# Graph attention and a routed feed-forward on one core: degrees by way of DRAM, and two pairs of heads at once in the graph layers

## The chip, the core and the metric

The kernel runs on one core of a Trainium2 chip. The metric is the time of one execution on the device in microseconds (us), as a median of several. Engines are named as the profile names them: PE (TensorE, its weight loads PEld), DVE (VectorE), ACT (ScalarE), POOL (GpSimd) and SP (SyncE, which here only issues DMAs). Each engine runs its own list of instructions strictly in order and waits on semaphores for the others.

## What is computed

Sixteen batches of 256 tokens of width 128 go through an attention block with a graph network in it, and then through a mixture of eight experts of which each token takes two. All is float32.

```python
xn = layer_norm(layernorm(x), gamma_in)
q, k, v = (xn @ Wq) * scale, xn @ Wk, xn @ Wv        # 16 heads of 64
attn = softmax(causal(q @ k.T))
out  = attn @ v
adj  = clip(attn + eye, 0, 1)
deg  = adj.sum(-1)
feats = v
for l in range(2):
    h = adj @ (feats @ gnn_w[l] + gnn_b[l]) / deg
    feats = gelu(h + feats)
out = out + feats @ lin_w + lin_b
x = x + layer_norm(out @ Wo, gamma_out)
# then: x + alpha * (top-2 of 8 experts: silu(gate) * up, down) of rmsnorm(layernorm(x))
```

The graph matrix that the kernel uses is adj / deg. Since only the diagonal of adj differs from attn, the attention output is recovered from the mixed values: attn @ v = deg * ((adj / deg) @ v) - (something on the diagonal), which the kernel arranges as (mixed values minus v) times the degree.

## The kernel before

**Stages.** A prologue loads the weights and splits them into high and low parts. Then one batch after another goes through `batch(b, before, routed, after)`: b is the batch in hand, `before` the batch whose attention output is being finished and normalised (b-1), `routed` the one whose tokens are sent to the experts' slots in DRAM (b-2), `after` the next, whose input is normalised. Batches 0, 1 and 15 are written out, 2 to 14 are a loop on every engine (`Fori`). Last, `sorted_stage` runs the experts over 71 tiles of sorted tokens, and the results are fetched and added.

**A batch.** Its 16 heads are 8 pairs n; a pair's two heads lie on the two halves of the partitions. Per pair: PE projects queries and keys (`queries_keys`), then `scores` (two banks of a rotation of three: `scores(n)` waits for `exps(n-1, 0)`); DVE takes the row maxima (`maxima`); ACT takes exponentials with their sums (`exps`); DVE puts in the diagonal and sums the degree parts (`adjacency`, then the reciprocal in `weights`); POOL scales the rows (`graph`, lines 497 and 499); PE transposes the result (`transposes`), ACT copies it to SBUF (`graph` on ACT, gt0 and gt1).

**Mixed values and degrees.** `differences` on PE multiplies the graph matrix with the values into the left half of bank 5. For the degree POOL multiplies den and rs, each value spread over 64 columns (`degrees`, line 508: 128x256 outputs a pair, tile deg), and PE transposes that with two 128x128 transposes (`degrees`, line 774) into the right half of bank 5. DVE then makes dT = bank - vT (`difference`, L1435) and aT = bank * dT (`attended`, L1440), and ACT copies the mixed values (`mixed_values`, gvT). Each of these has 256 columns.

**The two graph layers.** Again pair by pair with 256 columns in a bank: `layer1` (PE), `layer1_out` (DVE, adds vT, L1455), `gelu1` (ACT), `layer2_in` (PE, four instructions of 128 columns), its copy (ACT, g1), `layer2` (PE), `layer2_out` (DVE, adds f1T, L1461), `gelu2` (ACT), `output_graph` (PE). The first tiled step of the output, `output_start`, and `output_attended` go into bank 7 with `output_graph`; `output_bias` and `output_kept` (DVE) take it out, with `output_natural` (PE) between.

**The order** is written out by hand in one `batch` function for each engine. Nothing plans it at run time: a call that isn't ready holds all that is behind it on its engine. The page's line 635 is the helper that issues every product; groups are told apart by their tiles.

**DVE's small steps** are spread between: `norm_step` 0 to 5 (next batch's input), `norm_tokens` 0 to 11 (batch before), `choose`, `place_tokens` (routing), and in the last batch `table_first` and `gate_up_high` (the experts' weights, whose low parts are POOL's `gate_up_low`).

**SP** issues the loads, then 33 DMAs that fill the slots in DRAM with zeros (line 364), then the experts' weights, and nothing between there and the last batch's loads.

Of the kernel before, what the change touches and what calls it, by code (L numbers as in the profile page):

```python
# [19 lines left out]
P = 128  # L20
BATCHES, TOKENS, DIM = 16, 256, 128
HEADS, DHEAD = 16, 64
PAIRS = HEADS // 2
TILES = TOKENS // P
# [48 lines left out]
def build_program(nc, x, wq, wk, wv, wvT, gnn_w, gnn_b, lin_wT, lin_b, wo, gamma_in, gamma_out,  # L73
                  norm_w, routerT, guT, downT, alpha, slots, pairs, out):
# [9 lines left out]
    with ctx:  # L84
# [26 lines left out]
        sq4 = sb("sq4", [P, TILES, DIM])  # L111
# [12 lines left out]
        zero = sb("zero", [P, CLEAR * ROW])  # L124
# [35 lines left out]
        gu_lo = sb("gu_lo", [P, EXPERTS, 2 * HID], f32r)  # L160

# [18 lines left out]
        deg = at("deg", [P, 3, 4, DHEAD])  # L180
# [4 lines left out]
        gvT = at("gvT", [P, PAIRS, TOKENS])  # L185
        vT = at("vT", [P, PAIRS, TOKENS])
        aT = at("aT", [P, PAIRS, TOKENS])
        f1T = at("f1T", [P, 4, TOKENS])
        g1 = at("g1", [P, 2, TILES, P])
        dT = at("dT", [P, TOKENS])  # L190
        z1 = at("z1", [P, 2, TOKENS])
        z2 = at("z2", [P, 2, TOKENS])
        f2T = at("f2T", [P, 4, TOKENS])
# [14 lines left out]
        xn = at("xn", [P, TILES, DIM])  # L208
# [48 lines left out]
        p_deg = Signal(sem("p_deg"), PAIRS)  # L257
# [3 lines left out]
        a_d = Signal(sem("a_d"), PAIRS)  # L261
        d_d = Signal(sem("d_d"), PAIRS)
        s_deg = Signal(sem("s_deg"), PAIRS)
        d_a = Signal(sem("d_a"), PAIRS)

        s_f1, d_z1 = Signal(sem("s_f1"), PAIRS), Signal(sem("d_z1"), PAIRS)
        a_f1 = Signal(sem("a_f1"), PAIRS)
        s_g1, a_g1 = Signal(sem("s_g1"), PAIRS), Signal(sem("a_g1"), PAIRS)
        s_h2, d_z2 = Signal(sem("s_h2"), PAIRS), Signal(sem("d_z2"), PAIRS)
        a_f2, s_og = Signal(sem("a_f2"), PAIRS), Signal(sem("s_og"), PAIRS)  # L270
# [46 lines left out]
        L1_BANK, L2_IN_BANK, L2_BANK = 0, 2, 1  # L317
        MIX, DEG = slice(0, TOKENS), slice(TOKENS, 2 * TOKENS)
# [17 lines left out]
        def _(sp):  # L336
# [24 lines left out]

            sp.wait_ge(k_consts, 1)
            for r in range(0, SLOT_ROWS, CLEAR * P):
                sp.dma_start(slots[r:r + CLEAR * P, :].rearrange("(p r) d -> p (r d)", p=P),
                             zero[:, :]).then_inc(w_clear, 16)

# [7 lines left out]
            for e in range(EXPERTS):  # L374
                if e >= 2:
                    sp.wait_ge(k_gu_lo, e - 1)
                sp.dma_start(raw_gu[:, e % 2, :], guT[e]).then_inc(w_gu[e % 2], 16)
# [54 lines left out]
        def _(pool):  # L432
# [70 lines left out]
            def degrees(b, n):  # L503

                s = n % 3
                if n >= 3:
                    s_deg.wait(pool, b, n - 2)
# [1550 lines left out]
```

## Time and profile before

| | us |
|---|---|
| median of 3 runs | 1147.88 |
| lowest, highest | 1142.15, 1152.14 |
| the profiled execution | 1155.31 |
| its span, first to last instruction | 1153.4 |
| PE busy | 1071.1 (93%) |
| DVE busy | 884.1 (77%) |
| ACT busy | 803.4 (70%) |
| POOL busy | 500.3 (43%) |

The profiled execution is 0.65% above the median, and its span is 1.9 us less than its time. "Busy" is time covered by at least one instruction; matmuls overlap in the pipeline, so the mean duration of one is longer than the distance from one start to the next, and it is the distance between starts that tells what a step costs PE.

### The profile page before, as it was taken

The numbers are of one execution on the slowest core, as the hardware profiler recorded it, in microseconds if no ns is written. First come the engines' busy times: TensorE is split into PE (matmuls) and PEld (weight loads), VectorE is DVE, ScalarE is ACT, GpSimd is POOL, SyncE is SP. The second block draws the span as 40 slices with busy tenths as digits, with TensorE's granted clock in tenths as the row PEclk, the third lists the DMA queues.
The fourth block names the chain that finished last, engine by engine and source line by source line (L and its number), as shares of the span: only waits on it lengthen the run. The fifth ranks groups of instructions, "written<-read, shape, count | busy, mean of one in ns | idle before, by whom it ended". The sixth has DMA issues, their size and how long they took to land.

```text
span 1153.4 us, 28732 instructions
## 1 busy us (share of the span) xinstructions
PE 1071.1 (93%) x8576; PEld 854.7 (74%) x8576; DVE 884.1 (77%) x3760; ACT 803.4 (70%) x2351; POOL 500.3 (43%) x649
## 2 busy tenths in 40 slices
PE   4899999999999999999999999999999968898993
PEld 3777777777777777777777777777777747898993
DVE  3667797979797979797979797979797984565556
ACT  3668686868686868686868686868787735464551
POOL 3334244434343535353534353535353552544444
PEclk9899999999999999999999999999999988998997
DMA  6970000000000000000000000000000021222227
GB/s 192 405 260 2 1 2 11 1 10 1 10 1 11 1 10 0 10 0 10 0 10 0 10 0 10 0 10 0 10 0 10 2 78 44 56 57 61 59 61 226
DMA packets 37312, 47.43 MB, mean 41 GB/s; under 512 B 6009, under 2 KB 28539, under 8 KB 37200
## 3 DMA queue, kind: packets, MB, share of 16 engines
q1 hardware_dynamic: 32880, 37.81, 10.3%
q0 software_dynamic: 4320, 8.47, 2.2%
q14 instruction: 84, 0.69, 0.2%
q8 instruction: 28, 0.46, 0.2%
HBM read 18.14 MB, written 28.58 MB: 41 GB/s over the span
## 4 chain that ended last, share of the span: by engine, by line
PE 83%; DVE 6%; issue 3%; ACT 2%; SPq 2%; DMA 1%; another core or an unknown queue 1%; POOL 0%; DVEq 0%; POOLq 0%; ACTq 0%
PE bank L635 68%; PE bank L735 3%; PE bank L748 3%; PE bank L774 2%; PE bank L751 2%; PE bank L749 2%; PE bank L1006 2%; DMA x_all<-in_x 1%; PE bank L988 1%; DVE eb L1421 1%; DVE x_all L1995 1%; DVE got L1993 1%; DVE nmax L1406 0%; PE bank L783 0%
## 5 line engine op out<-in xcount | busy, mean ns | idle before, releaser
L497 POOL TENSOR_TENSOR ea<-ea,wgt 128x256 f32<-128x256 f32 x128 | 80.0, 625 | 429.6 <-DVE wgt L1430 396.1
L1406 DVE TENSOR_REDUCE nmax<-bank 128x1 f32<-128x128 f32 (+1 forms) x512 | 152.2, 347 | 66.0 <-PE bank L635 57.1
L499 POOL TENSOR_TENSOR eb<-eb,wgt 128x512 f32<-128x512 f32 x128 | 133.6, 1044 | 0.0
L635 PE MATMUL bank<-gt,g 128*64 128x256 f32 (+1 forms) x1024 | 112.0, 339 | 19.5 <-DVE z L1461 12.0
L1421 DVE SCALAR_TENSOR_TENSOR eb<-idw,ssum,eb 128x256 f32<-128x256 f32 x256 | 129.8, 544 | 0.0
L1124 ACT ACTIVATE ea<-bank,nmax 128x128 f32<-128x128 f32 x256 | 95.8, 374 | 47.9 <-DVE nmax L1406 45.9
L1124 ACT ACTIVATE eb<-bank,nmax 128x256 f32<-128x256 f32 x256 | 123.4, 482 | 0.0
L1092 ACT ACTIVATE gt<-bank 128x512 f32<-128x512 f32 (+1 forms) x256 | 111.7, 493 | 13.3 <-PE bank L751 11.8
L635 PE MATMUL bank<-gt,vnat 128*64 128x256 f32 (+1 forms) x1024 | 110.0, 335 | 3.0 <-issue 0.8
L635 PE MATMUL bank<-qk 64*128 64x128 f32 (+1 forms) x1024 | 112.7, 339 | 0.0
L525 POOL DMA_INDIRECT pairs<-zout,zin x71 | 69.7, 981 | 99.0 <-DVE zout L1954 89.3
L635 PEld LDWEIGHTS bank<-gt,g 128*64 128x64 f32 x1024 | 66.5, 137 | 61.4 <-issue 35.4
L1092 ACT ACTIVATE g<-bank 128x256 f32<-128x256 f32 x128 | 48.8, 381 | 84.8 <-PE bank L635 84.8
L635 PEld LDWEIGHTS bank<-gt,vnat 128*64 128x64 f32 x1024 | 65.1, 136 | 50.2 <-issue 17.0
L1461 DVE TENSOR_TENSOR z<-bank,f1T 128x256 f32<-128x256 f32 x128 | 53.6, 419 | 48.5 <-PE bank L635 48.5
L635 PE MATMUL bank<-xt_lo,w_hi 128*128 128x256 f32 x256 | 87.0, 340 | 1.9 <-DVE xt_lo L1399 1.9
L635 PE MATMUL bank<-gw,f1T 128*128 128x128 f32 x512 | 88.1, 295 | 0.3 <-ACT f1T L1148 0.3
L1947 DVE TENSOR_TENSOR shid<-bank,ssg 128x352 f32<-128x352 f32 x71 | 37.3, 525 | 63.5 <-ACT ssg L1272 40.6
L1092 ACT ACTIVATE qk<-bank 128x512 f32<-128x512 f32 x128 | 78.1, 610 | 11.2 <-PE bank L635 8.9
L635 PEld LDWEIGHTS bank<-gw,f1T 128*128 128x128 f32 x512 | 70.3, 192 | 19.3 <-issue 11.0
L1418 DVE SCALAR_TENSOR_TENSOR ea<-ident,ssum,ea 128x128 f32<-128x128 f32 x256 | 83.2, 362 | 0.0
L1092 ACT ACTIVATE gvT<-bank 128x256 f32<-128x256 f32 x128 | 49.1, 383 | 44.2 <-DVE aT L1440 40.6
(234 smaller groups left out, 3153.0 us busy)
## 6 DMA issues: line engine op xcount, KB each, us to landing
slots<-zero SPq DMA_DIRECT2D x33, 520.0 KB, 15.0
zin<-slots SPq DMA_DIRECT2D x71, 65.0 KB
got<-pairs SPq DMA_DIRECT2D x8, 512.0 KB, 5.5
raw_gu<-in_guT SPq DMA_DIRECT2D x8, 352.0 KB, 3.0
out<-x_all SPq DMA_DIRECT2D x8, 256.0 KB, 2.7
pairs<-zout,zin POOLq DMA_INDIRECT x71
dn<-in_downT SPq DMA_DIRECT2D x2, 512.0 KB, 16.0
slots<-z,row_now POOLq DMA_INDIRECT x64
```

The source lines that it names most:

```text
L497: nc.gpsimd.tensor_tensor(ea[:, s], ea[:, s], wgt[:, s, 0:2].unsqueeze(2).to_broadcast([P, 2, P]), ALU.mult)
L499: nc.gpsimd.tensor_tensor(eb[:, s], eb[:, s], wgt[:, s, 2:4].unsqueeze(2).to_broadcast([P, 2, 2 * P]), ALU.mult).then_inc(p_g.sem, 1)
L525: nc.gpsimd.indirect_dma_start(pairs, bass.IndirectOffsetOnAxis(ap=zin[:, j % RING, ID:ID + 1].bitcast(u32), axis=0), zout[:, j % RING, :] ...
L635: return nc_mm(o, st, mo, start=first, stop=last, **more)
L735: mm = nc.tensor.transpose(o[:, m * TOKENS + t * P:m * TOKENS + (t + 1) * P], vnat[:, t, n * P:(n + 1) * P], ident[:, :])
L1092: return nc.scalar.activation(o, i, ACT.Copy, **more)
L1124: done = nc.scalar.activation(e[:, s, a, :], score_bank(n, a)[:, TILE_SCORES[t]], ACT.Exp, bias=nmax[:, s, i:i + 1], accum_out=ssum[:, s, ...
L1406: done = V.tensor_reduce(nmax[:, n % 3, i:i + 1], score_bank(n, a)[:, TILE_SCORES[t]], X, ALU.max, negate=True)
L1418: V.scalar_tensor_tensor(ea[:, s, a, :], ident[:, :], ssum[:, s, a:a + 1], ea[:, s, a, :], ALU.mult, ALU.max, accum_out=den[:, s, a:a + 1])
L1421: done = V.scalar_tensor_tensor(eb[:, s, a, :], idw[:, :], ssum[:, s, 2 + a:3 + a], eb[:, s, a, :], ALU.mult, ALU.max, accum_out=den[:, s, ...
L1461: V.tensor_tensor(z2[:, n % 2, :], bank[L2_BANK][:, 0:TOKENS], f1T[:, n % 4, :], ALU.add).then_inc(d_z2.sem, 1)
L1947: V.tensor_tensor(shid[:, j % 2, 0:HID], bank[2 + j % 2][:, 0:HID], ssg[:, j % 2, :], ALU.mult).then_inc(d_hid.sem, 1)
```

## The change

1. **Degrees.** POOL multiplies four values a partition for a pair (tile dg) and no longer 256. SP writes them, two pairs (one "double") at a time, to a DRAM tensor `degs` as rows of 512 tokens, and reads each row back onto 64 partitions at once (tile dgb, four buffers). PE's transposes of deg and deg itself are gone. The product with the degree, `attended`, now has both its inputs in SBUF (aT and dgb), and runs in place.
2. **Doubles.** `differences`, `difference`, `attended`, `mixed_values`, `layer1`, `layer1_out`, `gelu1`, `layer2_in`, `layer2`, `layer2_out` and `gelu2` each take two pairs, in a whole bank of 512 columns. The last double uses banks 4 and 3 in layer 2. As before, `layer2(d)` waits for `layer2_out(d-1)` whichever bank it writes.
3. **Order anew** on PE, ACT, DVE and POOL. DVE's `attended(0)` comes in the second half of the batch, `attended(1)` and `attended(2)` after the last `layer2_out`, and `attended(3)` in the next batch behind its first maxima; so `output_attended` 0 to 7 all go to the next batch. POOL's `deviation` and `degrees` come earlier or later, and its `token_power(before, 0)` after graph(7) and degrees(7).
4. **SP** issues 9 of the 33 zero fills at once and three more behind each of the first eight doubles; the degree DMAs of batches 2 to 15 follow the loads of the experts' weights 0 and 1, and those of weights 2 to 7 come after them.
5. Tiles: `zero` lies in gu_lo, xh is normalised in place (xn is gone), sq4 is gone, gvT has 4 pairs for 8.

```diff
-        deg = at("deg", [P, 3, 4, DHEAD])
+        dg = at("dg", [P, DOUBLES, 2, 2, TILES])
+        dgb = at("dgb", [P, DGB, 2 * TOKENS])
...
+            def degrees_out(k):
+                p_dg.wait(sp, k // DOUBLES, 2 * (k % DOUBLES) + 2)
+                sp.dma_start(degs[2 * k:2 * k + 2, :].rearrange("a (j p) -> p (a j)", p=P),
+                             dg[:, k % DOUBLES].rearrange("p a m t -> p (a m t)"),
+                             allow_slow_non_contiguous=True).then_inc(w_dg[k % 2], 16)
+            def degrees_in(k):
+                sp.wait_ge(w_dg[k % 2], 16 * (k // 2 + 1))
+                if k >= DGB:
+                    sp.wait_ge(d_a.sem, k - DGB + 1)
+                for a in range(2):
+                    sp.dma_start(dgb[a * DHEAD:(a + 1) * DHEAD, k % DGB, :],
+                                 degs[2 * k + a:2 * k + a + 1, :].to_broadcast([DHEAD, 2 * TOKENS])).then_inc(w_dgb[k % DGB].sem, 16)
+            def degrees(first, last):
+                for k in range(first, last):
+                    degrees_out(k)
+                    if k % DOUBLES:
+                        degrees_in(k - 1)
+                    if k % DOUBLES == DOUBLES - 1:
+                        degrees_in(k)
...
             def degrees(b, n):                                     # POOL
-                nc.gpsimd.tensor_tensor(deg[:, s], den[:, s, :].unsqueeze(2).to_broadcast([P, 4, DHEAD]),
-                                        rs[:, s, :].unsqueeze(2).to_broadcast([P, 4, DHEAD]),
-                                        ALU.mult).then_inc(p_deg.sem, 1)
+                nc.gpsimd.tensor_tensor(dg[:, n // 2, :, n % 2, :].rearrange("p a t -> p t a"),
+                                        den[:, s, :].rearrange("p (t a) -> p t a", t=TILES),
+                                        rs[:, s, :].rearrange("p (t a) -> p t a", t=TILES),
+                                        ALU.mult).then_inc(p_dg.sem, 1)
...
-            def differences(b, n):                                 # PE
+            def differences(b, d):
+                a_gt.wait(pe, b, 2 * d + 2)
+                if d >= 1:
+                    a_d.wait(pe, b, d)
+                for m in range(2):
+                    n = 2 * d + m
+                    mm = mixed(bank[5][:, m * TOKENS:(m + 1) * TOKENS],
+                               lambda t, a: vnat[:, t, n * P + a * DHEAD:n * P + (a + 1) * DHEAD], n)
+                mm.then_inc(s_mix.sem, 1)
-            def degrees(b, n):
-                p_deg.wait(pe, b, n + 1)
-                for t in range(TILES):
-                    mm = nc.tensor.transpose(
...
+            def layer2(b, d):
+                a_g1.wait(pe, b, d + 1)
+                if L2_BANKS[d] in (3, 4):
+                    a_gt.wait(pe, b, PAIRS)
+                if d >= 1:
+                    d_z2.wait(pe, b, d)
...
+            def attended(b, d):                                    # DVE
+                d_d.wait(dve, b, d + 1)
+                w_dgb[d].wait(dve, b, 32)
+                V.tensor_tensor(aT[:, 2 * d:2 * d + 2, :], aT[:, 2 * d:2 * d + 2, :],
+                                dgb[:, d % DGB, :].rearrange("p (n i) -> p n i", n=2), ALU.mult).then_inc(d_a.sem, 1)
```

PE's second part of the batch, as it now stands:

```diff
+                scores(b, 7)
+                places(routed, bank[7][:, PLACES], before)
+                differences(b, 1)
+                layer1(b, 0)
+                transposes(b, 5)
+                layer1(b, 1)
+                x_transposed(after, b)
+                output_start(b, before, routed)
+                layer2_in(b, 0)
+                differences(b, 2)
+                layer2(b, 0)
+                transposes(b, 6)
+                layer2_in(b, 1)
+                transposes(b, 7)
+                layer1(b, 2)
+                differences(b, 3)
+                layer2(b, 1)
+                output_graph(b, 0)
+                layer1(b, 3)
+                output_graph(b, 1)
+                layer2_in(b, 2)
+                queries_keys(after, 0, b)
+                output_graph(b, 2)
+                layer2_in(b, 3)
+                layer2(b, 2)
+                layer2(b, 3)
+                tokens_transposed(before, bank[6], after)
+                queries_keys(after, 1)
+                output_graph(b, 3)
+                values(after, 0, b)
```

DVE, from the seventh pair's maxima on:

```diff
+                weights(b, 5)
+                maxima(b, 7, 0)
+                take_places(routed, bank[7][:, PLACES])
+                maxima(b, 7, 1)
+                place_tokens(routed, 0)
+                place_tokens(routed, 1)
+                difference(b, 1)
+                norm_tokens(before, 0)
+                layer1_out(b, 0)
+                norm_step(after, 5)
+                adjacency(b, 6)
+                adjacency(b, 7)
+                weights(b, 6)
+                norm_tokens(before, 1)
+                layer1_out(b, 1)
+                difference(b, 2)
+                weights(b, 7)
+                layer2_out(b, 0)
...
+                layer2_out(b, 3)
+                attended(b, 1)
+                attended(b, 2)
```

## Rows read from the trace of the kernel before

**Rows 1.** Busy time by stretch: length, then PE, PEld, DVE, ACT, POOL, PEclk, DMA, GB/s
```profile
195.94:252.90 56.96, 56.10 (x464) 43.17 (x464) 47.63 (x217) 43.71 (x134) 24.95 (x33) 1.00 0.02 5
...
824.40:881.40 57.00, 56.13 (x465) 43.19 (x464) 47.63 (x217) 43.75 (x134) 24.96 (x33) 1.00 0.02 5
...
541.96:570.96 29.00, 28.89 (x259) 22.46 (x258) 25.51 (x123) 25.12 (x85) 10.49 (x15) 1.00 0.00 1
570.96:599.00 28.04, 27.28 (x209) 20.78 (x209) 22.10 (x95) 18.66 (x49) 14.48 (x19) 1.00 0.03 10
```

**Rows 2.** PE in order of time, one batch of the loop: start, duration, instruction
```profile
562.57 0.88 PE L635 MATMUL bank<-qk 64*128 64x128 f32 x8
563.38 0.39 PE L635 MATMUL bank<-xt_lo,w_hi 128*128 128x256 f32 x1
...
564.28 0.87 PE L635 MATMUL bank<-gt,vnat 128*64 128x256 f32 x8
...
573.25 0.33 PE L748 MATMUL bank<-ident,ea 128*128 128x128 f32 x1
...
573.96 0.60 PE L635 MATMUL bank<-gvT,gw 128*128 128x256 f32 x2
574.40 0.38 PE L774 MATMUL bank<-ident,deg 128*128 128x128 f32 x2
574.62 1.03 PE L635 MATMUL bank<-aT,wo_sb 128*128 128x256 f32 x4
575.48 0.68 PE L635 MATMUL bank<-gw,f1T 128*128 128x128 f32 x4
576.04 0.70 PE L635 MATMUL bank<-aT,wo_sb 128*128 128x256 f32 x2
...
577.10 0.87 PE L635 MATMUL bank<-gt,vnat 128*64 128x256 f32 x8
577.80 0.82 PE L635 MATMUL bank<-gt,g 128*64 128x256 f32 x8
578.55 0.71 PE L635 MATMUL bank<-gw,f1T 128*128 128x128 f32 x4
```

**Rows 3.** DVE in order of time, same batch, and past the loop's end
```profile
540.75 0.43 DVE L1461 TENSOR_TENSOR z<-bank,f1T 128x256 f32<-128x256 f32 x1 [1.94 <-PE bank L635]
543.73 1.15 DVE L1406 TENSOR_REDUCE nmax<-bank 128x1 f32<-128x128 f32 x4 [2.55 <-PE bank L635]
...
572.54 0.41 DVE L1455 TENSOR_TENSOR z<-bank,vT 128x256 f32<-128x256 f32 x1
...
885.21 1.15 DVE L1406 TENSOR_REDUCE nmax<-bank 128x1 f32<-128x128 f32 x4 [1.83 <-PE bank L635]
```

**Rows 4.** Instructions on tile x_all: min/median/max ns, first and last start
```profile
L1995 DVE TENSOR_TENSOR x_all<-x_all,got x6: 691/692/2062, 1137.8 to 1148.9; 128x512 f32<-128x512 f32 x6
```

**Rows 5.** DVE and POOL in order of time: one held instruction and its neighbour
```profile
578.10 1.25 DVE L1421 SCALAR_TENSOR_TENSOR eb<-idw,ssum,eb 128x256 f32<-128x256 f32 x1
...
579.28 0.48 DVE L1421 SCALAR_TENSOR_TENSOR eb<-idw,ssum,eb 128x256 f32<-128x256 f32 x1
...
579.69 0.41 DVE L1455 TENSOR_TENSOR z<-bank,vT 128x256 f32<-128x256 f32 x1
580.02 0.41 DVE L1461 TENSOR_TENSOR z<-bank,f1T 128x256 f32<-128x256 f32 x1
...
577.99 1.08 POOL L499 TENSOR_TENSOR eb<-eb,wgt 128x512 f32<-128x512 f32 x1
```

**Rows 6.** DMA issues by line: KB each, median us to landing
```profile
slots<-zero SPq DMA_DIRECT2D x33, 520.0 KB, 15.0
...
gb<-in_gnn_b SPq DMA_DIRECT2D x4, 0.2 KB, 2.3
```

**Rows 7.** The last batch's longest wait on PE, and ACT's table load
```profile
931.39 1.55 PE L635 MATMUL bank<-gt,g 128*64 128x256 f32 x8 [5.10 <-DVE z L1461]
...
573.59 1.28 ACT L1148 ACT_TABLE_LOAD   x1
```

More of the change, by code:

```diff
@@ L565, in batch @@
                         scatter(routed, c)
+                graph(b, 6)
+                graph(b, 7)
                 degrees(b, 6)
-                graph(b, 7)
                 degrees(b, 7)
-                if after is not None:
-                    deviation(after, 1, 7)
+                if before is not None:
+                    token_power(before, 0)
                 if after is None:
-                    for e in range(0, 3):
+                    for e in range(0, 2):
                         gate_up_low(e)
@@ L796, in layer2_in @@
-            def layer2_in(b, n):
-                a_f1.wait(pe, b, n + 1)
-                if n >= 1:
-                    a_g1.wait(pe, b, n)
-                for t in range(TILES):
-                    mm = product(bank[L2_IN_BANK][:, xt(t)], f1T[:, n % 4, xt(t)], gw[:, 1, :], True, True)
-                mm.then_inc(s_g1.sem, 1)
-            def layer2(b, n):
-                a_g1.wait(pe, b, n + 1)
-                if n >= 1:
-                    d_z2.wait(pe, b, n)
-                mixed(bank[L2_BANK][:, 0:TOKENS],
-                      lambda t, a: g1[:, n % 2, t, a * DHEAD:(a + 1) * DHEAD], n).then_inc(s_h2.sem, 1)
+                    d_z1.wait(pe, b, d)
@@ new lines, in layer1, with layer2_in @@
+                for m in range(2):
+                    mm = product(bank[L1_BANK][:, m * TOKENS:(m + 1) * TOKENS], gw[:, 0, :], gvT[:, 2 * (d % 2) + m, :],
+                                 True, True)
+                mm.then_inc(s_f1.sem, 1)
+            def layer2_in(b, d):
+                a_f1.wait(pe, b, d + 1)
+                if L2_IN_BANKS[d] in (3, 4):
+                    a_gt.wait(pe, b, PAIRS)
+                if d >= 1:
+                    a_g1.wait(pe, b, d)
+                for i in range(2 * TILES):
+                    mm = product(bank[L2_IN_BANKS[d]][:, xt(i)], f1T[:, d % 2, xt(i)], gw[:, 1, :], True, True)
+                mm.then_inc(s_g1.sem, 1)
@@ L870, in batch @@
                     folded_lin(1)
+                if before is not None:
+                    output_graph(before, 6)
+                    output_attended(before, 3)
                 scores(b, 4)
-                differences(b, 1)
+                transposes(b, 1)
                 if before is not None:
-                    output_natural(before)
-                degrees(b, 1)
+                    output_graph(before, 7)
+                    output_attended(before, 4)
                 queries_keys(b, 6)
@@ L880, in batch @@
                 scores(b, 5)
+                differences(b, 0)
+                transposes(b, 3)
+                if before is not None:
+                    output_attended(before, 5)
+                scores(b, 6)
+                if before is not None:
+                    output_attended(before, 6)
+                    output_attended(before, 7)
                 queries_keys(b, 7)
-                differences(b, 2)
+                transposes(b, 4)
+                if before is not None:
+                    output_natural(before)
@@ L1252, in tokens_transposed @@
+                if after is not None:
+                    values(after, 0)
             def tokens_transposed(p, o):
```

569 lines of the change are left out of this document (238 added, 331 removed).

## The prediction

> **What bounds the kernel now.** I read the stretches by batch first. Batches of the loop are alike: from 195.94 to 881.40 us there are 12, 57.12 us each, and in each PE is busy for 56.1, DVE 47.6, ACT 43.8, POOL 25 [rows 1]. The clock is granted in full (1.00, 2.4 GHz) throughout, so it is no lever. PE is the bound, by its own work and not by a chain; sixteen batches make some 920 of the 1153 us, and the change touches nothing else but the start and the passage to the experts. Then the two parts of a batch: from `scores(0)` to the end of `scores(7)` (541.96 to 570.96, 29.0 us) DVE is busy for 25.5; in the rest (28.0 us) for 22.1 [rows 1]. So DVE is close behind PE in the first part: `layer1_out(1)` starts at 572.54, 1.6 us after `scores(7)` ended [rows 3]. A change that makes PE's batch shorter runs into DVE soon. That decides this case.
>
> **What PE saves.** Degree transposes: two of them move the next start by 0.22 us (574.40 to 574.62) [rows 2]; their mean of 0.28 each is overlap and not what they cost. Eight pairs: 8 x 0.22 = 1.8 us a batch. Doubles: a mixed group of eight costs 0.70 where another follows (577.10 to 577.80) and 0.75 where another kind does; after queries and keys the distance from the last start is longer still [rows 2]. The new order has 12 such runs of narrow groups where the old has 16. At 0.05 to 0.3 a run I take 0.2, 0.8 us in all. `layer2_in` doesn't gain: four instructions cost 0.56 (575.48 to 576.04) [rows 2] and eight will cost 1.1; nor does `layer1`, 0.44 each. PE's own need is 56.1 - 1.8 - 0.8 = 53.5 us.
>
> **What the others save.** One 512-column instruction for two of 256. On DVE two steps follow at 0.33 (579.69 to 580.02) [rows 5], a mean of 0.42; one of 512 columns takes 0.69 [rows 4], 0.61 from start to start. So 32 of 0.34 become 16 of 0.61: 10.9 to 9.8 us, 1.1 a batch. ACT saves some 3 us and POOL, whose degree product shrinks from 256 outputs to 4, some 3 more (bounds 0 and 5); neither is the bound at 44 and 25 of 57 [rows 1], so I count nothing for them.
>
> **DVE's walk through the new order** (0 is the start of `scores(0)`). Before, from the first maximum to `layer1_out(1)` passed 572.54 - 543.73 = 28.8 us [rows 3], of which DVE idled 29.0 - 25.5 - 1.77 (its late start) = 1.7 [rows 1, 3]: 27.1 of work. The new order takes out of this stretch nine 256-column steps (3.1) and a norm step (0.4), and puts in `difference(0)`, `attended(3)` of the batch before (1.2) and three norm steps (1.3): 26.1. With small waits of 0.4, 26.5.
>
> When does it start? Before, the last step of a batch ended at 541.18 and the first maximum began at 543.73, 2.55 us later, though its scores ended at 542.96; past the loop's end the same wait was 1.83 [rows 3]. I read the 2.55 as the price of DVE's own turn of the loop. It was hidden, for DVE's last step ended before `scores(0)` began. Now `attended(1)` and `attended(2)` stand between the last `layer2_out` and the turn, 1.2 us more. PE does 2.2 us (tokens, queries and keys, graph output, values) between the end of `layer2(3)` and `scores(0)`; `layer2_out(3)` takes 0.6 to 0.7 of these; so DVE begins at -1.5 + 1.2 + 2.55 = 2.2 us, where it was 1.77. Then maxima(7) end at 2.2 + 26.5 = 28.7; behind them come `place_tokens` (0.9), `difference(1)` (0.6), `norm_tokens(0)` (0.4) and `layer1_out(0)` (0.6): 31.2. With `output_kept`, for which `places` waits, and the held small steps, 31.7.
>
> PE's work up to `layer1(1)`, which waits for that: eight scores at 0.93 (the 0.81 of 562.57 to 563.38 and the masks' 0.12) 7.4, six projections at 0.85 5.1 (563.38 to 564.28 is 0.90), values 2.4, value transposes 1.8, six `transposes` at 0.71 (573.25 to 573.96) 4.2, twelve output products at 0.43 (574.62 to 575.48 are two) 5.2, two double differences 3.0, `layer1(0)` 0.9, small ones 0.7: 30.7 [rows 2]. So PE waits there about 1.0 us.
>
> **After `layer1(1)`** PE has: six double mixed groups (`differences` 2 and 3, `layer2` 0 to 3) at 1.5 each (0.70 + 0.80) 9.0; `transposes` 6 and 7 1.4; three `layer1` 2.6; four `layer2_in` 4.4; output graph 1.7; projections and values of the next batch 2.3; start of output and two transposed pairs 1.1 [rows 2]: 22.5. New stalls: `layer2(3)` stands right behind `layer2(2)` but waits for `layer2_out(2)`, drain, 0.69 [rows 4] and hand-over, 0.85 us; `layer2_in(0)` waits for a table load of 1.28 [rows 7] and gelu, over which PE has 1.8 of work, 0.3; `differences(3)` waits for POOL's graph(7), transposes and ACT's copy, 0.1 or 0.2. Together 23.9. POOL's `token_power(before, 0)` now stands behind graph(7): DVE's `norm_tokens(2)` waits for it some 1.3 us, covered since `layer1_out(2)` can't start before `layer1(2)`. `transposes(6)`, for which POOL must first be through with its four scatters, has 0.4 to 1 us of room.
>
> **Sum.** 31.7 + 23.9 = 55.6, say 55.7 us a batch against 57.12: 1.4 less. Thirteen turns of the loop: 18. Batches 0 and 1 have no turn and less DVE work, 1.8 each (the transposes): 3.6. Start: DVE waits for x either way, one adjacency fewer stands before the second pair's maxima: 1. The last batch: before, PE lost 5.10 us in one wait for `layer2_out` [rows 7]. Now `attended` 1 to 3, `table_first(4)` behind `gate_up_high(7)` and SP's loads behind the last degrees come late; between a gain of 5 and a loss of 10 I take a loss of 3. Total -20 us (18 + 4 + 1 - 3). The profiled execution's 1155 would become 1135; from the median of 1147.9 I forecast 1128 us, own range 1116 to 1142.
>
> **DMAs.** A double's degrees leave as 512 elements of 4 bytes. No row shows that many; bounds are 2.3 us (64 elements) and 15.0 (520 KB behind others) [rows 6]. I take 3 to 4 for the write and 3 for the read, 7 with issue. SP is idle in between, and issues 12 a batch at some 0.5. `attended(3)` has the least room: degrees(7) are there some 7.5 us after `layer1(1)` starts, it is wanted at 3 to 4 of the next batch, 19 us later. The others have as much or more. The 24 zero fills spread over batches 0 and 1 delay only reads with that room. Nothing counted.
>
> **A rule of the skill that speaks against the change.** A DVE step that began at 578.10 beside POOL's 577.99 product took 1.25 us where the next of its kind, at 579.28, took 0.48: it was held [rows 5]. The Trainium skill, "SBUF — State Buffer", on which engine shares which port, says that a DVE instruction with two SBUF inputs and a GpSimd instruction that reads SBUF exclude each other for the whole of one of them. The trace agrees, with 0.77 us lost. Before, `attended` read a bank; now both its inputs are in SBUF. From the row alone: one of the four, `attended(0)`, stands beside a product of POOL, +0.8 us where DVE isn't last; the other three are beside an idle POOL. I count nothing, and the held steps go into a rival.
>
> **Rivals.**
> 1. *PE stays the bound.* If the 2.55 us are a wait for something else, or DVE catches up, the batch comes to 53.5 plus 0.85 and little else, 54.3: 2.8 x 13 = 36, + 5 - 3: 1110; without any stall 1100. For it: 1.7 us of idle DVE in the first part, and ACT's and POOL's relief. Against: 26.5 us of DVE work in a PE stretch of 27 to 28. I give 1104. Chance 0.18.
> 2. *DVE gives it all back.* Held steps (the 0.77), a turn of 2.85, exps late behind the table load: 1.2 to 1.4 us more per batch on the path to `layer1_out(0)`. Then 57 us a batch, and 1147. Chance 0.20.
> 3. *The degrees come late* (the slower side). Place: `attended(3)`, at the head of DVE's batch, with maxima and everything behind it. It decides from a round trip of 19 us on; each microsecond over is one per batch. Two landings near 10 us, with issue 21 to 22, give 2.5 x 15 = 37 on top of 1128: 1165. Elements of 4 bytes speak for it, an otherwise empty queue (DMA share 0.02 [rows 1]) against. With longer DVE chains of the same effect, chance 0.13.
>
> **Numbers.** Forecast 0.49. About 1% (11 us) is what a measurement here tells from no change, so faster means below 1136. Of the forecast 0.42 lies there, of rival 1 all, nothing of the others: 0.60. Same: 0.07 + 0.19 = 0.26. Slower: 0.14. The range 1098 to 1152 leaves out rival 3 and the edges.
>
> **What will show it.** In the profile after: a loop batch of 55 to 56.5 us, PE busy 53 to 54; L774 gone; DVE's 512-column steps at 0.69; a PE wait for z of L1455's successor (`layer1_out(0)`) near 1 us and one for `layer2_out(2)` near 0.85 in each batch; the first maxima 2 us or more after `scores(0)` began. Wrong if `attended` waits for DMA, if DVE idles over 2 us in the first part, or if the batch is under 54.5 or over 57.

## The result, and the profile after

The changed kernel takes 1211.24 us (median of 4 runs, 1205.77 to 1215.33) against 1147.78 (4 runs): the ratio is 1.0549, 95% interval [1.05, 1.0598]. The forecast was 1128 us, with a range of 1098 to 1152; the kernel became slower and not faster, and its time lies outside the range. The profiled execution has a span of 1207.3 us against 1153.4. The kernel before was measured anew beside each group of runs below (medians of 1145.99 to 1154.04 us), and each ratio is against that; medians of different groups can differ by some 0.5% for that reason alone.

First the page of the changed kernel: the busy row, then the DMA rows (packets, MB, share of the 16 engines over the span).

```profile
PE 1030.5 (85%) x8320; PEld 833.0 (69%) x8320; DVE 859.0 (71%) x3504; ACT 767.4 (64%) x2095; POOL 444.9 (37%) x649
DMA packets 114053, 63.99 MB, mean 53 GB/s; under 512 B 74617, under 2 KB 97147, under 8 KB 114000
q1 hardware_dynamic: 109680, 54.87, 34.9%
q0 software_dynamic: 4320, 8.47, 6.3%
q14 instruction: 26, 0.21, 0.1%
```

The same DMA rows of the kernel before:

```profile
DMA packets 37312, 47.43 MB, mean 41 GB/s; under 512 B 6009, under 2 KB 28539, under 8 KB 37200
q1 hardware_dynamic: 32880, 37.81, 10.3%
q0 software_dynamic: 4320, 8.47, 2.2%
q14 instruction: 84, 0.69, 0.2%
```

No engine does more work than before. What grew is the number of packets: 64 doubles of 1024 pieces of 4 bytes are 65,536, nearly all of the 68,600 more below 512 B. And the scatters' queue (q0), with the same 4320 packets, is three times as busy.

Where the 53.9 us went, by the starts of `scores(0)` (the first `mask,pick` row of a batch on TensorE): up to batch 3 217.4 us against 198.7 (+18.7); the 12 batches from there 58.62 each against 57.12 (+18.0); from batch 15 to the end 286.6 against 269.2 (+17.4). A third in each.

The loop first. Two of its batches in their two parts, up to `scores(7)` and from there, as in [rows 1] (columns: stretch, length, then PE, PEld, DVE, ACT and POOL busy, clock, DMA share, GB/s):

```profile
507.69:535.73 28.04, 26.71 (x223) 20.78 (x223) 23.50 (x119) 23.09 (x78) 9.77 (x15) 1.00 0.02 0
535.73:566.26 30.53, 26.36 (x225) 20.72 (x226) 23.17 (x83) 18.43 (x41) 11.77 (x18) 1.00 0.71 36
566.26:596.06 29.80, 26.72 (x223) 20.78 (x223) 23.50 (x119) 23.10 (x78) 9.76 (x15) 1.00 0.04 9
596.06:629.47 33.41, 27.68 (x226) 21.50 (x227) 22.08 (x83) 18.30 (x41) 11.74 (x18) 0.95 0.59 40
```

PE is busy for 53.1 us of the first batch (53.5 were forecast), DVE for 46.7. The batches are no longer alike: 58.6 and 63.2 us here, 55.6 to 63.2 over the loop. DMA engines that had a share of 0.02 over a batch [rows 1] have 0.6 to 0.7 in the second part. TensorE's clock plays a small part: it is granted in full (2.4 GHz) in the whole loop before, and in the changed kernel but for three stretches of 3.4 us at half (1.2 GHz), which is why the last row has 0.95. They lie in the three longest batches (61.8, 63.2 and 62.7 us), and the one in the rows, from 597.3 to 600.7, follows a wait of TensorE of 2.9 us. By an estimate from these figures they cost 1.7 us each at most, 5 of the 36 us that the loop takes more than in the run without the DMAs below.

Now TensorE's waits for VectorE in the first of these batches, and the first maximum of the next:

```profile
541.15 1.10 PE L664 MATMUL bank<-gvT,gw 128*128 128x256 f32 x4 [0.73 <-DVE z L1471]
562.61 1.52 PE L664 MATMUL bank<-gt,g 128*64 128x256 f32 x16 [0.88 <-DVE z L1479]
567.31 0.62 DVE L1417 TENSOR_REDUCE nmax<-bank 128x1 f32<-128x128 f32 x2 [1.25 <-PE bank L664]
```

`layer1(1)` waits 0.73 us for `layer1_out(0)` (forecast 1.0) and `layer2(3)` 0.88 for `layer2_out(2)` (forecast 0.85). VectorE's first maximum comes 1.05 us after `scores(0)` began and not at 2.2, with 1.25 of idle time in place of the 2.55 of [rows 3]. So the two foreseen waits of TensorE are there in about their size. The lost time is elsewhere, in the list of waits (us in total, times, longest):

```profile
DVE aT L1455 <- DMA dgb<-degs: 21.8, 6, 10.6
POOL ea L525 <- DMA slots<-gu_lo: 18.1, 1, 18.1
DVE gu_hi L1486 <- DMA raw_gu<-in_guT: 17.6, 4, 15.7
DVE z L1479 <- remote: 16.1, 9, 3.3
DVE nmax L1417 <- remote: 14.6, 8, 3.4
ACT gt L1115 <- remote: 12.9, 7, 3.1
```

and in SyncE's own:

```profile
SPq L367 <- POOL dg L535: 501.7, 32, 21.4
SPq L376 <- DMA degs<-dg: 192.5, 33, 11.7
```

A write of degrees (L367) lands up to 11.7 us after SyncE begins to wait for it; 3 to 4 us were forecast. The first three waits of the engines belong to the start and the end: `attended` of the first batches for late degrees, the first scatter (for which GpSimd holds `ea`) for zero fills (their source tile is now `gu_lo`) that SyncE issued between degrees, and the last batch for gate and up weights that stand behind the last degrees in SyncE's queue. Those with the releaser "remote" are the loop's for the most part: the profile writes this where a signal came but no instruction that gives it had ended in the 1.5 us before. Here is the largest, in order of time:

```profile
589.12 0.28 PE L664 MATMUL bank<-mask,pick 64*128 64x128 bf16 x4
589.24 0.87 PE L664 MATMUL bank<-qk 64*128 64x128 f32 x8
589.83 0.69 DVE L1447 TENSOR_TENSOR aT<-bank,vT 128x512 f32<-128x512 f32 x1
593.87 1.15 DVE L1417 TENSOR_REDUCE nmax<-bank 128x1 f32<-128x128 f32 x4 [3.35 <-remote]
594.53 0.37 ACT L1147 ACTIVATE ea<-bank,nmax 128x128 f32<-128x128 f32 x1 [4.06 <-DVE nmax L1417]
595.47 0.44 PE L811 MATMUL bank<-ident,yT 128*128 128x128 f32 x2 [2.93 <-DVE yT L1460]
```

`scores(6)` is through at 590.1, and VectorE, free from 590.5, takes the maxima at 593.9. A second place, 17 us on:

```profile
606.33 1.47 PE L664 MATMUL bank<-gt,g 128*64 128x256 f32 x16
608.22 0.38 PE L784 MATMUL bank<-ident,eb 128*128 128x128 f32 x2
610.96 0.69 DVE L1479 TENSOR_TENSOR z<-bank,f1T 128x512 f32<-128x512 f32 x1 [3.19 <-remote]
611.03 0.87 ACT L1115 ACTIVATE gt<-bank 128x512 f32<-128x512 f32 x2 [2.71 <-remote]
```

`layer2(0)` ended at 607.8 and `transposes(6)` at 608.6; VectorE and ScalarE, which wait for them, both start at 611.0. All lines of this kind in the loop are waits for a group of TensorE. The kernel before has none in its loop.

The trace also has the time of each semaphore signal, and it tells on which side the delay is. For the first place: four groups of TensorE ended at 590.1, 591.2, 591.9 and 592.5, and their signals are recorded at 593.85, 593.91, 593.98 and 594.06, all within 0.21 us and in the order of the groups. From 200 to 880 us, 50 of TensorE's 702 recorded signals come more than 1 us after the end of their group, the worst 3.7 us; of the 1773 signals of VectorE, ScalarE and GpSimd none comes later than 0.02 us. So VectorE starts at once when its signal comes, and TensorE's signals come late (or its matmuls end late: the ends in the profile are modelled).

### The profile page after: what moved, and what is told of

Same layout as the page of the kernel before. It is cut to its first block, busy times and chain, and to the rows that moved or that the text cites. A ratio compares the mean times of both kernels' runs of the same rounds, so it can differ in the third digit from the quotient of the medians.

```text
span 1207.3 us, 27665 instructions
## 1 busy us (share of the span) xinstructions
PE 1030.5 (85%) x8320; PEld 833.0 (69%) x8320; DVE 859.0 (71%) x3504; ACT 767.4 (64%) x2095; POOL 444.9 (37%) x649
## 3 DMA queue, kind: packets, MB, share of 16 engines
q0 software_dynamic: 4320, 8.47, 6.3%
## 4 chain that ended last, share of the span: by engine, by line
issue 41%; POOL 18%; PE 17%; DMA 15%; DVE 3%; SPq 3%; ACT 1%; POOLq 0%; another core or an unknown queue 0%; DVEq 0%; ACTq 0%
PE bank L664 13%; DMA slots<-z,row_now 7%; POOL eb L527 7%; POOL slots L547 4%; POOL ea L525 3%; DMA degs<-dg 3%; PE bank L1024 2%; POOL rstd L519 1%; POOL dg L535 1%; SPq L376 1%; DMA dgb<-degs 1%; DMA pairs<-zout,zin 1%; DMA x_all<-in_x 1%; DMA zin<-slots 1%; DMA raw_gu<-in_guT 1%
## 5 line engine op out<-in xcount | busy, mean ns | idle before, releaser
L664 PE MATMUL bank<-gt,g 128*64 128x256 f32 (+1 forms) x1024 | 98.4, 335 | 19.5 <-DVE z L1479 16.8
L1433 DVE SCALAR_TENSOR_TENSOR eb<-idw,ssum,eb 128x256 f32<-128x256 f32 x256 | 113.5, 480 | 0.0
L664 PE MATMUL bank<-gt,vnat 128*64 128x256 f32 (+1 forms) x1024 | 100.8, 341 | 6.2 <-ACT gt L1115 3.6
L664 PE MATMUL bank<-gw,f1T 128*128 128x128 f32 x512 | 71.1, 282 | 26.2 <-ACT g L1115 21.6
L1479 DVE TENSOR_TENSOR z<-bank,f1T 128x512 f32<-128x512 f32 x64 | 43.9, 686 | 64.9 <-PE bank L664 48.8
L664 PEld LDWEIGHTS bank<-gw,f1T 128*128 128x128 f32 x512 | 65.2, 193 | 32.5 <-ACT f1T L1174 25.1
L664 PE MATMUL bank<-aT,wo_sb 128*128 128x256 f32 x256 | 80.5, 410 | 7.3 <-DVE aT L1455 7.3
L781 PE MATMUL bank<-ident,ea 128*128 128x128 f32 x256 | 66.2, 286 | 18.0 <-ACT gt L1115 12.9
L1174 ACT ACTIVATE f1T<-z,gb 128x512 f32<-128x512 f32 x64 | 46.1, 721 | 55.6 <-DVE z L1471 47.2
L664 PE MATMUL bank<-gvT,gw 128*128 128x256 f32 x256 | 69.4, 394 | 13.5 <-DVE z L1471 9.4
```

Source lines behind the costliest of these rows:

```text
L664: return nc_mm(o, st, mo, start=first, stop=last, **more)
L781: nc.tensor.transpose(bank[3][:, a * TOKENS:a * TOKENS + P], ea[:, s, a, :], ident[:, :])
L1174: nc.scalar.activation(f1T[:, d % 2, :], z1[:, d % 2, :], ACT.Gelu, bias=gb[:, 0:1]).then_inc(a_f1.sem, 1)
L1433: done = V.scalar_tensor_tensor(eb[:, s, a, :], idw[:, :], ssum[:, s, 2 + a:3 + a], eb[:, s, a, :], ALU.mult, ALU.max, accum_out=den[:, s, ...
L1479: V.tensor_tensor(z2[:, d % 2, :], bank[L2_BANKS[d]][:, :], f1T[:, d % 2, :], ALU.add).then_inc(d_z2.sem, 1)
```

## The experiments

In each diff "-" is the changed kernel's line, unless said otherwise.

**Without the DMAs.** Does the new order hold what it promised?

```
-                    degrees_out(k)
-                    if k % DOUBLES:
-                        degrees_in(k - 1)
...
-                w_dgb[d].wait(dve, b, 32)
```

> The changed kernel without any of its 192 degree DMAs: attended multiplies by a tile of ones that is set once, and waits for no DMA (the output lacks the degrees). Theory A (the degree DMAs do the harm: their many 4-byte pieces hold up whatever else goes through the same DMA engines, and with it DVE and ACT, whose idle stretches of 1.2 to 3.4 us have no engine as releaser): a loop batch falls from 58.6 to 55.5 to 56.5 us, the stretches before maxima(6) and layer2_out(0) go, and with the start and the last batch mended the time is near 1125. Theory B (the new order and the doubles are slow by themselves, the stretches belong to the loop's own code): the loop batch stays at 58 or above and only start and end are mended, some 1180.

Measured: 1131.96 us (2 runs), ratio 0.9822 [0.9744, 0.99]. The twelve batches from batch 3 on are alike to 0.03 us; one of them:

```profile
468.26:523.83 55.57, 52.81 (x448) 41.50 (x448) 46.38 (x201) 41.48 (x118) 21.53 (x33) 1.00 0.01 5
```

55.57 us where 55.7 were forecast. The 79 us between the changed kernel and this run are due to the DMAs of the degrees.

**The same DMAs in the kernel before** (of a spare tile, for batches 2 to 14; its degree transposes stay):

```
+            for k in range(8, 60):
+                degrees_out(k)
+                if k % 4:
...
+                    degrees_in(k - 1)
```

> The kernel before with the same DMAs beside it in batches 2 to 14: for each double one write of 1024 pieces of 4 bytes and two reads of 128 KB onto 64 partitions, of a spare tile, for which no engine waits but SP. Theory A: the loop batch of the old order grows from 57.1 by 1.5 to 3 us, time 1165 to 1185. Theory B: it stays within 0.3 us of 57.1, time within 1% of before.

Measured: 1236.37 us, ratio 1.0728 [1.062, 1.0836]: more than expected. Its loop batches take 63.2 us in place of 57.1, and its waits say "remote" as well (35.8 us at `nmax`, 24.2 at `z`). The old order suffers more, 6.1 us a batch against 3.0; why isn't shown. The harm needs no degree that comes late, for nothing reads them here.

**128 pieces of 32 bytes.**

```
-                sp.dma_start(degs[2 * k:2 * k + 2, :].rearrange("a (j p) -> p (a j)", p=P),
+                sp.dma_start(degs[2 * k:2 * k + 2, :].rearrange("a (q f) -> (a q) f", f=8),
```

> The changed kernel, whose writes of degrees go out as 128 runs of 32 bytes and not as 1024 of 4 bytes (the reads are the same in size and number, the values land in another order, so the output is another). Theory A in its narrow form (it is the number of tiny pieces): loop batch near 56, time 1140 to 1160, since the round trip is short in the first batches and the last too. If the reads (256 KB a double) or the round trip itself do it, the loop batch stays over 58.

Measured: 1138.61 us, ratio 0.988 [0.979, 0.9969]; loop batches 55.85. The 128 reads of 128 KB are still there: they are not the cause.

**Writes only.**

```
-                        degrees_in(k - 1)
+                        sp.wait_ge(w_dg[(k - 1) % 2], 16 * ((k - 1) // 2 + 1))
...
-                w_dgb[d].wait(dve, b, 32)
+                Signal(w_dg[d % 2], 32).wait(dve, b, 16 * (d // 2 + 1))
```

> The changed kernel with the writes of 4-byte pieces left as they are and the broadcast reads left out; attended waits for the landing of its write and multiplies by ones, so the output lacks the degrees. Theory A1 (the 1024 small pieces of a write do the harm alone): 1180 to 1215 us, with the same idle stretches of VectorE at the maxima of pair 6. Theory A2 (they do it only where they meet the reads and scatters): 1132 to 1160 us.

Measured: 1206.3 us, ratio 1.0495 [1.0436, 1.0554]: theory A1. The writes do it, without the reads. The queues of this run from 524 to 566 us:

```profile
q0 software_dynamic: 128, 0.27, 20.1%
q1 hardware_dynamic: 4160, 0.02, 4.5%
```

and of the run without degree DMAs from 540 to 600:

```profile
q0 software_dynamic: 128, 0.27, 1.3%
```

The 128 packets of four scatters keep the engines busy for 0.201 x 42 = 8.4 us of their time in place of 0.013 x 60 = 0.8. The 4096 pieces themselves take only 1.9: it is others that they make slow.

**Other sizes.** 256 pieces of 16 bytes, with the broadcast row read at a stride by `attended`; 512 of 8 bytes likewise:

```
+                sp.dma_start(degs[2 * k:2 * k + 2, :].rearrange("a (p f) -> p a f", p=P),
+                             dg[:, k % DOUBLES].rearrange("p a m t -> p a (m t)")).then_inc(w_dg[k % 2], 16)
...
+                now = aT[:, 2 * d:2 * d + 2, :].rearrange("p n (t i) -> p n t i", t=TILES)
+                V.tensor_tensor(now, now, dgb[:, d % DGB, :].rearrange("p (i n t) -> p n t i", n=2, t=TILES),
```

> The changed kernel with each double's degrees written as 256 pieces of 16 bytes instead of 1024 of 4 bytes; DRAM then holds them token by token, the broadcast reads are as before, and attended takes the degrees at a stride of 4 elements. It computes all that the reference does. Theory A (what costs is the number of small pieces): near the run with 128 pieces of 32 bytes, 1135 to 1150 us. Theory B (what costs is that pieces below some size, here under 32 bytes, are slow each): half or more of the loss stays, over 1165 us. The strided operand of attended could cost up to 0.7 us a double if it halves VectorE's rate, which would show as a mean of 1.3 us in place of 0.68.

> The changed kernel with each double's degrees written as 512 pieces of 8 bytes, the point between 1024 pieces (1211 us) and 256 pieces (1133 us). If the harm grows with the number of pieces in proportion beyond those of 16 bytes: (512 - 256) / (1024 - 256) of the 78 us, 1159 us. If there is a limit above which the transfers no longer hide: below 1140 or above 1180 us.

Measured: 16 bytes 1132.8 us, ratio 0.9878 [0.9844, 0.9912]; 8 bytes 1138.13 us, 0.9872 [0.9845, 0.9898]. Not in proportion: 512 pieces of 8 bytes and 256 of 16 cost little, 1024 of 4 bytes cost 79 us. With 16 bytes `attended` reads the degrees at a stride of four elements, with 8 bytes at a stride of two. Their rows:

```profile
L1455 DVE TENSOR_TENSOR aT<-aT,dgb 128x512 f32<-128x512 f32 x64 | 69.0, 1100 | 0.0
L1455 DVE TENSOR_TENSOR aT<-aT,dgb 128x512 f32<-128x512 f32 x64 | 42.7, 690 | 0.0
```

The stride of four made it slower, 1100 ns in place of 684, and the batch is 55.84 us in place of 55.57; the stride of two cost `attended` nothing (690).

**Turned on TensorE first**, so that a double leaves as 8 rows of 512 bytes:

```
+                nc.tensor.transpose(bank[4][0:8 * (last - first), 2 * P:3 * P],
+                                    dg[:, first:last].rearrange("p d a m t -> p (d a m t)"),
```

> The changed kernel with the degrees turned on TensorE first (3 transposes of 128 columns a batch, into the free part of bank 4, copied by ScalarE into a tile of 16 partitions), so that a double's degrees leave as 8 rows of 512 bytes. It computes all that the reference does. Theory A (pieces): no waits for DMA in the loop, batches of 55.8 plus up to 0.9 us (3 transposes of 0.3 on TensorE), in all 1132 to 1150 us. If instead the transfers harm by being there at all, whatever their pieces: over 1165 us.

Measured: 1146.07 us, ratio 0.999 [0.9973, 1.0006]. The pieces are gone and so is the gain: batches are 56.3 us (0.7 more than without DMAs, which three transposes may explain), and `attended` waits 17.3 us in all for degrees that take one more stage.

**Number, size or place?**

```
(512 of 4 bytes)    degs[2 * k:2 * k + 1, :] ... dg[:, k % DOUBLES, 0]
(8 bytes, twice)    the write of 8 bytes, and once more to rows 2 * (k + BATCHES * DOUBLES)
(64 bytes apart)    degs[k % 2:k % 2 + 1, :].rearrange("o (j p s) -> p (o j) s", p=P, s=16)[:, :, 0]
(8 bytes apart)     the same with s=2
```

> As the run with writes only (no reads, attended multiplies by ones, so the output lacks the degrees), with only one head's half of each double's degrees written: 512 pieces of 4 bytes in place of 1024 (1206 us). If their number in a write has a limit between 512 and 1024: 1128 to 1145 us. If it is the size of 4 bytes, each piece with its own cost: half the harm, near 1169 us.

> The kernel with 512 pieces of 8 bytes, with each double's degrees written twice, to two places of DRAM: 1024 pieces in two writes. If the number of pieces is what harms: as with 1024 of 4 bytes, over 1180 us. If the size of 4 bytes does: within 10 us of 1138.

> As the run with writes only, the 1024 pieces of 4 bytes lying 64 bytes apart in DRAM in place of side by side (attended multiplies by ones, so the output lacks the degrees). If neighbours that fall into the same few bytes of DRAM hold each other up: under 1160 us. If each piece of 4 bytes costs by itself wherever it lies: 1195 to 1215 us.

> As the run with writes only and pieces 64 bytes apart, with the 1024 pieces of 4 bytes 8 bytes apart (the output lacks the degrees). If only two pieces that share 8 bytes of DRAM hold each other up: 1122 to 1135 us. If it is enough to share 64 bytes: 1160 to 1210 us.

| a double's writes | us | ratio, interval | batch of the loop |
|---|---|---|---|
| 1024 x 4 B side by side, no reads | 1206.3 | 1.0495 [1.0436, 1.0554] | 59.6 |
| 512 x 4 B side by side, no reads | 1174.45 | 1.0238 [1.0194, 1.0282] | 57.9 |
| 1024 x 8 B side by side, with reads | 1132.17 | 0.9867 [0.9842, 0.9892] | 55.58 |
| 1024 x 4 B, 8 bytes apart, no reads | 1127.04 | 0.9826 [0.9794, 0.9858] | 55.58 |
| 1024 x 4 B, 64 bytes apart, no reads | 1126.57 | 0.9822 [0.9795, 0.985] | 55.56 |

The table has the answer. The run with 8 bytes twice has more packets than the changed kernel, by its page,

```profile
DMA packets 115078, 64.26 MB, mean 57 GB/s; under 512 B 75641, under 2 KB 98171, under 8 KB 115024
```

and by the row of one of its batches

```profile
468.85:524.43 55.58, 52.82 (x448) 41.53 (x448) 46.36 (x201) 41.51 (x118) 21.55 (x33) 1.00 0.20 24
```

ten times the DMA share of the old loop; yet it has no wait labelled "remote" there. So it is not the number of packets alone, nor the 4 bytes alone: pieces of 4 bytes that touch, two to each 8 bytes of DRAM, do the harm, and half as many of them do some 60% of it (47 of 79 us above 1127). Two things are not told apart. Pieces that share 8 bytes also touch each other, so either could be the condition. And the runs with gaps write the same two rows again and again, where the others write a new place each time; that alone isn't the remedy, since the writes of 8 and 16 bytes go to new places too and do no such harm.

**The start and the end.**

```
-            pieces, ahead = SLOT_ROWS // (CLEAR * P), 9
+            pieces, ahead = SLOT_ROWS // (CLEAR * P), 33
```

> The changed kernel with all 33 zero fills issued ahead of the first degrees, as before. If the loss up to batch 3 (18.7 us) comes from degrees and fills taking turns in SyncE's queue, the wait of the scatter for the fills (18.1 us) goes and the wait of attended for the first degrees stays or grows: 5 to 15 us less than the changed kernel, 1197 to 1206. If it comes from the pieces themselves, within 4 us of it, or slower, since the first degrees then queue behind all 33 fills (some 130 us).

Measured: 1213.26 us, ratio 1.051 [1.0477, 1.0543], no gain. GpSimd's wait of 18.1 us went, and another came, in the first 140 us:

```profile
DVE aT L1455 <- DMA dgb<-degs: 20.3, 1, 20.3
```

So the order of the fills only decides who waits. The loss needs the slow writes: with 16 or 32 bytes and nine fills ahead, the same stretch up to batch 3 takes 191.7 and 191.3 us, against 217.4 in the changed kernel and 214.4 here.

```
-            for e in range(2, EXPERTS):
-                sp.wait_ge(k_gu_lo, e - 1)
...
+                    nc.gpsimd.dma_start(raw_gu[:, e % 2, :], guT[e + 2]).then_inc(w_gp[e % 2], 16)
```

> The changed kernel with the gate and up weights of experts 2 to 7 loaded from GpSimd's queue, each behind the subtraction that frees its buffer, instead of from SyncE's queue behind the last degrees. If the wait of 15.7 us for them in the last batch is due to their place in SyncE's queue: 12 to 17 us less than the changed kernel, 1193 to 1200 us, and no wait of ScalarE's copies (21.6 us) there. If it's due to busy DMA engines: within 4 us of the changed kernel.

Measured: 1198.35 us, ratio 1.0456 [1.0417, 1.0495], 13 less than the changed kernel. From batch 15 to the end it takes 268.4 us, 18 less; TensorE's 21.6 us of waiting for ScalarE's copy in that batch, which came from the 15.7 of `gu_hi`, are 7.7 now, and those of `gu_hi` 2.1 at most. SyncE's queue was the cause there. (The stretch up to batch 3 was 9.9 us longer in this profile and the loop 4.4 shorter, without an edit to either.)

**TensorE's own wait.**

```
                 if L2_BANKS[d] in (3, 4):
                     a_gt.wait(pe, b, PAIRS)
-                if d >= 1:
+                    d_z2.wait(pe, b, d - 1)
+                elif d >= 1:
                     d_z2.wait(pe, b, d)
```

> The changed kernel in which layer2(3), which writes bank 3, waits for layer2_out(1) and no longer for layer2_out(2). I expect PE's wait of 0.88 us there to go in each loop batch; if PE is what ends a batch the batch shortens by 0.5 to 0.9 (time 8 to 12 us less, 1200), if DVE's chain does, by less than 0.3.

Measured: 1204.38 us, ratio 1.045 [1.0328, 1.0573]; against the changed kernel's 1211 too near to tell, though its loop batches are 57.64 us against 58.62. So once more on top of the pieces of 16 bytes, and with the loads on GpSimd's queue besides:

> The kernel with pieces of 16 bytes, and layer2 of the last double (bank 3) no longer waits for layer2_out of the double before it (bank 1), only for the one before that. In the run with pieces of 16 bytes this wait is 0.9 us of each batch. If TensorE's waits add up one by one: 13 times 0.9, so 11 to 12 us less than 1132.8, near 1121. If VectorE's chain to the next batch's scores sets the end of the batch all the same: within 3 us of 1132.8.

> As the run with pieces of 16 bytes and layer2 freed, and the gate and up weights of experts 2 to 7 loaded from GpSimd's queue. In the run with pieces of 16 bytes VectorE waits for these loads 3 us at most in the last batch, so if the 13 us that this edit gave with pieces of 4 bytes were the queue behind slow degrees, it gives 0 to 3 us here; if they were the place of the loads alone, some 10 us.

Measured: 1121.82 us, ratio 0.9727 [0.9705, 0.975], and 1123.39 us, 0.9742 [0.9721, 0.9763]. They can't be told apart. The first has the lowest median of the kernels that compute everything, 2.7% below the one before. One of its batches:

```profile
462.46:517.30 54.84, 52.52 (x447) 41.36 (x446) 48.09 (x202) 41.61 (x118) 21.57 (x33) 1.00 0.09 24
```

1.0 us less than without the edit, 12 over the twelve: the wait of 0.9 us that was taken from TensorE is won in full here. The loads give nothing once the degrees are quick, so their 13 us were the queue behind slow writes, and not their place.

## Why the prediction was wrong, and where it was right

**The step that failed** is the paragraph on DMAs, "A double's degrees leave as 512 elements of 4 bytes ... I take 3 to 4 for the write and 3 for the read, 7 with issue ... Nothing counted". The count was wrong (2 rows of 512 are 1024 elements). The read was right (median 3.3 us). The write was not: in the loop its last signal is recorded 7.6 to 17.5 us after its issue, the median is 11.5, and 4.5 in the run whose pieces lie 8 bytes apart (some signals are missing from the record, so these are lower bounds). More than that, the paragraph priced a transfer by its landing alone. This write makes the scatters' packets beside it slow and comes with late signals of TensorE, and neither of the two rows that served as bounds has such pieces. The sum had nothing there, and the runs show 79 us. Against the run without these DMAs, by the spans: 27 up to batch 3 (217.4 against 190.4), 36.5 in the loop (3.04 a batch), 14 from batch 15 on (286.6 against 272.5). All three signs of being wrong that the prediction names came true: batches over 57 us, `attended` waiting for a DMA, and VectorE idle for over 2 us in the first part of a batch (4.5 in the first of the rows above, 28.04 less 23.50).

**Rival 3** had the side and the cause (pieces of 4 bytes) but not the place. In the whole loop `attended` waits for degrees once, 1.0 us; the other 20.8 are in batches 0 and 1. For `attended(3)` the round trip, from the issue of the write to the landing of the read, was forecast at 7 us and takes 13.6 to 18.5 in the loop, just under the rival's threshold of 19; in batches 0 and 1 it is 26.5 and 20.9, and there `attended` waits, `attended(2)` most (10.6 and 4.7 us). Its 1165 was too low, since it let the DMAs hurt only those who wait for them.

**What was right**, by the runs without the harm (55.57 and 55.58 us a batch against 55.7):
- TensorE's need of 53.5 us: 52.8 busy.
- `layer1(1)` begins 31.8 us after `scores(0)` (forecast 31.7) and 24.1 more follow (23.9), in the run with 16 bytes. The first is in part luck: VectorE starts 1.15 us earlier than forecast, and then waits 1.5 us for TensorE at the maxima of pairs 1 and 2, where 0.4 of small waits were counted.
- The stalls: `layer1(1)` 0.73 (1.0), `layer2(3)` 0.89 (0.85), `layer2_in(0)` 0.40 (0.3). `transposes(6)`, to which 0.4 to 1 us of room was given, waits 0.46 for GpSimd.
- The batches up to the loop gain 8.3 us (6 forecast, with batch 2), and the end loses 3.3 in the run without DMAs (3 forecast). That last term can't be checked closer: the same stretch takes 265 to 277 us in the runs with only the writes changed.

**The turn of the loop** was misread. Before, VectorE's first maximum began 0.7 to 1.1 us after `scores(0)` had ended; in the changed kernel it begins 0.06 us after, so its 1.25 us of idle time are a wait for TensorE and not a price of the turn. In the run with 16 bytes, where `attended(1)` and `attended(2)` take 0.8 us longer, only 0.45 of them are left: the turn now costs that at most, where 2.55 were charged. The page's instruction queue (q14) had four to six packets in each batch of the loop before, about the turn, some 5 us ahead of it and in the middle; in the changed kernel, whose loop is shorter by 16 instructions on each of TensorE, VectorE and ScalarE, there was one in twelve batches. It looks as if a loop no longer has to be loaded anew; no run tests that alone.

**The rule on the shared port** (the Trainium skill, "SBUF — State Buffer", under "Who interferes with whom") was put against one `attended` of the four. None of the 64 was held:

```profile
L1455 DVE TENSOR_TENSOR aT<-aT,dgb x64: 678/684/693, 70.8 to 1008.6; 128x512 f32<-128x512 f32 x64
```

That doesn't contradict the rule: in the batch of the rows above, GpSimd's last product ended at 550.4 and `attended(0)` began at 551.4. In runs whose degrees come sooner one `attended` was held, in batch 0; here with 8 bytes, where it began at 65.52 beside a product of GpSimd that ran to 66.08:

```profile
L1455 DVE TENSOR_TENSOR aT<-aT,dgb x64: 677/683/1105, 65.5 to 934.7; 128x512 f32<-128x512 f32 x64
```

It took 0.42 us more than the median. The trace agrees with the rule, once in 64 and not once in four.

## What to carry to other kernels

Count the pieces of every DMA and look where neighbours lie: a transposing write of 4-byte values makes pieces that touch, and most of its price is paid by others. Keep two values together (8 bytes) and let the reader take the stride; here a stride of two cost VectorE nothing, and one of four 0.4 us an instruction. And price a DMA that joins a queue by what stands behind it, at the start and the end of the kernel above all.

## What the hardware showed beyond that

- **Starts 4 bytes apart do harm, 8 do not.** 1024 pieces of 4 bytes: 1206 us side by side, 1127 with 8 bytes from one to the next, 1127 with 64. The Trainium skill, "DMA: Bandwidth & Descriptors", under Specifications, has line rate only from 512 B, and read-modify-write below. All these pieces are below it, and those of 8 bytes, and those that lie apart, do no such harm, so that rule alone doesn't give what was measured. The same page's rules for kernel authors say that a non-contiguous last dimension lowers to one descriptor per element; the trace agrees (68,600 more packets below 512 B for 65,536 pieces of 4 bytes).
- **The clock falls behind the waits.** Between batches 3 and 15 the granted clock fell to half, for 3.4 or 6.8 us at a time, in each of the seven kernels with touching pieces of 4 bytes (3 to 7 times) and in none of the other eleven.
- **A delay with idle DMA engines.** At 590.5 VectorE begins to wait for 3.35 us. The DMA engines did nothing from 585 to 600; two rows of that (share in the last column but one):

```profile
592.00:593.00 1.00, 0.54 (x5) 0.30 (x3) 0.00 (x0) 0.00 (x0) 0.00 (x0) 1.00 0.00 0
593.00:594.00 1.00, 0.00 (x0) 0.00 (x0) 0.13 (x1) 0.00 (x0) 0.00 (x0) 1.00 0.00 0
```

But a write was still open. It had been issued at 582.6, its packets are recorded from 583.0 to 584.5, and its landing signals only from 591.96 to 593.99; TensorE's four signals came from 593.85 to 594.06. An idle share of the DMA engines doesn't say that a write is through.

What is shown: such waits at `nmax`, `z` and `gt` are in the loops of all seven kernels that write neighbours of 4 bytes, the changed one among them, and of none of the other eleven. From 200 to 880 us these seven have 31 to 73 signals of TensorE that are over 1 us late; the run without degree DMAs, both runs with gaps, the one with 8 bytes twice, the one with 16 bytes and the one with rows of 512 have none, and the kernel before has two. In the changed kernel 28 of the 50 late signals come within 0.15 us of a landing signal of such a write, but only 71 of the 652 others.

Four runs with larger pieces (8, 16 and 32 bytes) have one wait of 2.3 to 2.6 us at ScalarE's copy of `layer2_in(0)` in nearly each batch; there too it is TensorE's signal that is recorded late, by 1.7 to 2.2 us. It costs little (55.9 us a batch against 55.6 with 8 and 32 bytes), and the first run with 16 bytes, which has the same writes, doesn't have it.

What is not shown: by which way a write holds up these signals.
